# Eight wide matmuls first, then eight narrow ones, in each output tile of the first product

## The reference, cut to what matters

```python
w = weight[adapter_ids]                       # (8, 1024, 1024), one matrix for each of 8 sequences
c = jnp.einsum('bsi,boi->bso', x, w)          # the first product: x (8, 256, 1024)
logits = c @ W_router.T                       # 8 experts, softmax, top 2, renormalised: combine
h = jnp.einsum('nd,erd->ner', c, A_stack) * combine[..., None]
lora = jnp.einsum('ner,eor->no', h, B_stack) * SCALING
out = x + c @ W_base.T + b_base + lora        # all float32
```

## Time and profile before

| | us |
|---|---|
| median of 3 runs | 419.95 (419.89 to 420.39) |
| profiled execution, its own time | 421.21 |
| its span, first to last instruction | 419.4 |
| TensorE busy | 407.3 (97%) |
| wide matmuls L798, 512 of them | mean 405 ns |
| narrow matmuls L800, 512 of them | mean 283 ns |
| DVE busy | 303.9 (72%) |
| ACT busy | 187.5 (45%) |

### The profile page before, as it was taken

The page is one execution under the profiler, slowest core; times in us unless marked ns, Lnnn a source line. Parts: engine busy times, 40 slices in busy tenths (PEclk is TensorE's granted clock), DMA queues, the critical chain, the costliest instruction groups (busy, mean ns, idle before and its releaser), DMA issues.

```text
span 419.4 us, 5350 instructions
## 1 busy us (share of the span) xinstructions
PE 407.3 (97%) x2010; PEld 341.9 (82%) x2010; DVE 303.9 (72%) x435; ACT 187.5 (45%) x289; POOL 39.8 (9%) x67
## 2 busy tenths in 40 slices
PE   7589999999999999999999999999999999999996
PEld 6478888888888888888888888888888888888885
DVE  2388794787979999877447688468877999987321
ACT  3387663474873234313126577246667224431100
POOL 8000000000000013012127000000000002201110
PEclk9689999999999999999999999999999999999999
DMA  7999685065813015467549959416444202631221
GB/s 238 363 362 324 207 288 187 31 221 166 299 38 100 2 75 168 159 210 273 185 168 322 391 174 327 157 60 198 146 161 155 86 2 80 197 127 50 100 77 75
DMA packets 21930, 72.84 MB, mean 174 GB/s; under 512 B 2912, under 2 KB 3952, under 8 KB 21904
## 3 DMA queue, kind: packets, MB, share of 16 engines
q1 hardware_dynamic: 16704, 56.11, 39.6%
q0 software_dynamic: 4912, 15.87, 10.7%
q10 hardware_dynamic: 288, 0.52, 0.4%
HBM read 64.10 MB, written 8.39 MB: 173 GB/s over the span
## 4 chain that ended last, share of the span: by engine, by line
PE 94%; DMA 3%; SPq 1%; DVE 0%; issue 0%; ACT 0%
PE bank_x L798 28%; PE bank_x L800 14%; PE bank_y L774 9%; PE bank_y L776 8%; PE bank_y L775 8%; PE bank_x L774 7%; PE bank_x L776 7%; PE bank_x L775 7%; DMA raw<-w_cond 3%; PE bank_y L813 2%; PE bank_y L814 2%; SPq L332 1%; PE bank_y L837 0%; SPq L344 0%; PE bank_y L829 0%
## 5 line engine op out<-in xcount | busy, mean ns | idle before, releaser
L798 PE MATMUL bank_x<-x_hl,wc_hl 128*128 128x512 f32 x512 | 185.3, 405 | 7.6 <-DVE wc_hl L648 5.9
L800 PE MATMUL bank_x<-x_hl,wc_hl 128*128 128x256 f32 x512 | 145.0, 283 | 0.0
L526 DVE TENSOR_TENSOR wc_hl<-raw,wc_hl 128x1024 fp32r<-128x1024 f32 x90 | 108.8, 1220 | 23.3 <-ACT wc_hl L452 23.3
L798 PEld LDWEIGHTS bank_x<-x_hl,wc_hl 128*128 128x128 f32 x512 | 97.8, 191 | 33.7 <-DVE wc_hl L648 6.5
L452 ACT CAST wc_hl<-raw 128x1024 fp32r<-128x1024 f32 x90 | 94.0, 1051 | 66.7 <-PE bank_y L776 34.8
L800 PEld LDWEIGHTS bank_x<-x_hl,wc_hl 128*128 128x128 f32 x512 | 98.5, 192 | 0.1
L406 POOL DMA_DIRECT2D out<-out_sb x28 | 15.3, 546 | 362.9 <-DVE out_sb L577 341.4
L569 DVE SCALAR_TENSOR_TENSOR out_sb<-bank_x,bias_sb,out_sb 128x512 f32<-128x512 f32 x32 | 23.8, 747 | 24.5 <-PE bank_x L776 19.1
L490 ACT COPY xc_low<-bank_x 128x256 f32<-128x256 f32 x64 | 23.7, 370 | 33.5 <-PE bank_x L800 33.5
L774 PE MATMUL bank_x<-x_hl,wc_hl 128*128 128x512 f32 x96 | 37.4, 389 | 0.0
L776 PE MATMUL bank_x<-x_hl,wc_hl 128*128 128x512 f32 x96 | 37.4, 389 | 0.0
(11 more groups left out here) (94 smaller groups left out, 511.2 us busy)
## 6 DMA issues: line engine op xcount, KB each, us to landing
raw<-w_cond SPq DMA_DIRECT2D x62, 512.0 KB, 4.5
raw<-w_base SPq DMA_DIRECT2D x24, 512.0 KB, 5.0
out_sb<-x POOLq DMA_DIRECT2D x32, 256.0 KB, 5.5
raw<-x SPq DMA_DIRECT2D x14, 512.0 KB, 4.5
out<-out_sb POOLq DMA_DIRECT2D x28, 256.0 KB, 2.3
raw<-w_cond SPq DMA_DIRECT2D x8, 128.0 KB, 7.2
out<-out_sb SPq DMA_DIRECT2D x4, 256.0 KB, 2.0
raw<-x ACTq DMA_DIRECT2D x2, 256.0 KB, 2.8
```

The costliest lines, as they stand in the source:

```text
L526: nc.vector.tensor_tensor(split_dst(key, LO), split_src(key), split_dst(key, HI).bitcast(F32), ALU.subtract).then_inc(lo_done, 1)
L798: nc.tensor.matmul(ps[:], wc_hl[:, w, HI, k], x_hl[:, s % 2, k].rearrange("p h n -> p (h n)"), start=(k == 0), stop=False)
L800: mm = nc.tensor.matmul(ps[:, TOK:], wc_hl[:, w, LO, k], x_hl[:, s % 2, k, HI], start=False, stop=(k == KT - 1))
```

## The change

In every tile but the first two, TensorE now waits only for the high part of the weights, does the eight wide matmuls, then waits for the low part, and does the eight narrow ones. The bank, the operands, the number of matmuls and weight loads and the increment at the end stay as they are. Tiles (0,0) and (0,1) keep their turns.

```diff
             def cond(s, t):
                 starts = s == 0 and t < 2
                 if not starts:
-                    pe.wait_ge(lo_done, SPLIT["w", s, t])
+                    pe.wait_ge(hi_done, SPLIT["w", s, t])
...
                     nc.tensor.matmul(ps[:], wc_hl[:, w, HI, k], x_hl[:, s % 2, k].rearrange("p h n -> p (h n)"),
                                      start=(k == 0), stop=False)
-                    mm = nc.tensor.matmul(ps[:, TOK:], wc_hl[:, w, LO, k], x_hl[:, s % 2, k, HI],
-                                          start=False, stop=(k == KT - 1))
+                    if starts:
+                        mm = nc.tensor.matmul(ps[:, TOK:], wc_hl[:, w, LO, k], x_hl[:, s % 2, k, HI],
+                                              start=False, stop=(k == KT - 1))
+                if not starts:
+                    pe.wait_ge(lo_done, SPLIT["w", s, t])
+                    for k in range(KT):
+                        mm = nc.tensor.matmul(ps[:, TOK:], wc_hl[:, w, LO, k], x_hl[:, s % 2, k, HI],
+                                              start=False, stop=(k == KT - 1))
                 mm.then_inc(cond_done, 1)
```

## The result

| | before | after |
|---|---|---|
| median of 6 runs, us | 420.46 (419.89 to 420.99) | 416.40 (416.06 to 416.75) |
| ratio | | 0.9904, 95% interval 0.9892 to 0.9917 |
| profiled execution, its own time | 421.21 | 416.06 |
| its span | 419.4 | 414.3 |

The change is worth 4.1 us. Predicted were 414.6 (411.0 to 418.8) and a gain of 5.4; the profiled pair is 5.15 apart, the medians 4.06. The prediction started from the median of the first three runs of before, 419.95. With three more it is 420.46, so of the 1.8 us between 414.6 and 416.40, 0.5 lies in the starting point and 1.3 in the gain.

A forecast was written before the change was run, and what follows sets the result against it. TensorE was taken as the bound: a start paced by loads and splits, then a stream of matmuls each costing its spacing. 1.27 + 0.81 + 0.28 + 3.0 = 5.4 us off the median 419.95 gave 414.6, range 411.0 to 418.8.

The forecast's parts named there:

- The wait of tile (0,2): In tile (0,2), wide matmuls start when the high part is made, not the low part: 1.27 us earlier.
- The clock: In tile (0,2), a busier TensorE avoids the half clock; half of 1.62 us taken, 0.81.
- The wait of tile (3,3): Ahead of tile (3,3), the wait for DVE's low part and the restart behind it go: 0.28 us.
- The order: In tiles behind (0,2), narrow behind narrow takes 0.120, so 56 tiles go from 2.827 to 2.773: 3.0 us.
- The added waits: Two waits per tile ahead of its loads, hidden by the running matmul, cost nothing; uncovered, 6.7 us for 61 tiles.
- From the profile to the median: Whole kernel: the same terms, 5.4 us, taken from the profiled 421.21 (415.8) and from the median 419.95 (414.6).
- weight loads that can't keep the pace: Narrow runs: loads of 0.19 stretch the spacing beyond 0.120; at 0.135 the kernel takes 421.9; chance 0.10.
- the quicker narrow spacing: Narrow runs: narrow behind narrow takes 0.113, a gain of 8.7 us in all, to 411.3; chance 0.17.
- The order does nothing: All reordered tiles: narrow ones keep 0.127, tiles stay at 2.83, gain 2.1 us, to 417.9; chance 0.25.

The follow-up runs named there:

- Experiment 4: Changed kernel with tile (0,2) waiting for the low part before its first matmul: bare, ratio 0.9951; with eight matmuls on zeros ahead of that wait, 0.9935.
- experiment 1: Changed kernel's matmul order in all 62 tiles, but each waits for the low part before its first matmul, as in the kernel before; ratio 0.9970.
- e8_late02: Changed kernel, except that tile (0,2) waits for the low part before its first matmul; ratio 0.9951.
- experiments 3 and 6: Kernel before plus eight matmuls on zeros ahead of tile (0,2), ratio 0.9996; kernel before plus one ahead of each of five tiles, one execution, no time given.
- experiments 2 and 3: Kernel before with only tile (0,2) in the new order and wait, 0.9966; kernel before plus eight matmuls on zeros ahead of (0,2), 0.9996.
- experiment 7: Kernel before with tiles (0,2), (3,3) wide first on the high part and a zero matmul ahead of five tiles, 418.30; changed kernel again beside it, 416.91.

## Why the prediction was right, and where its terms were off

The direction and the range held, and so did the mechanism: all four terms are there. Their sizes were right in two of them, and that the sum came close is partly luck. By its own steps, against the profiled pair (5.1 us of span):

- **The wait of tile (0,2), 1.27.** Held: it started at 22.00, released by L452, 1.45 before 23.45, of which 0.20 is that ACT's copy began earlier in this profile (20.90 for 21.10). Experiment 4 has 1.3 for it, sure to 1 us.
- **The clock, 0.81 as half of 1.62.** The pair has the whole of it: (0,3) starts 3.02 earlier, of which the two terms in full are 2.89. In the medians about half fits: 7 of 12 executions in experiment 1 and 4 of 10 in `e8_late02` lie in the upper heap. For the kernel before itself the share is not known, since its executions vary in the gait too. "Half" was a guess. The argument behind it, that TensorE would be busier ahead of the tile, fits the pair (3.19 of 3.80 us), but the clock also stayed in a profile with 1.14 (experiment 4), so it does not say when the clock falls.
- **The wait of tile (3,3), 0.28.** Held: (3,2) and (3,3) take 2.79 each and 0.31 less together than before, 0.01 of it by the order. DVE makes the low part of (3,3) by 102.41 (101.19 + 1.22), but the tile starts at 102.04, so 0.37 us of waiting are covered there by the wide matmuls:

```profile
101.19 1.22 DVE L526 TENSOR_TENSOR wc_hl<-raw,wc_hl 128x1024 fp32r<-128x1024 f32 x1 [0.52 <-ACT wc_hl L452]
102.04 0.86 PE L798 MATMUL bank_x<-x_hl,wc_hl 128*128 128x512 f32 x3
```

- **The order, 3.0.** This term was mis-sized: it measured 56 x (2.827 - 2.793) - 5 x 0.020 = 1.8, of it 1.1 in the 32 tiles of the second group, where 1.7 was forecast. The narrow spacing that it took, 0.120, was right (0.119 to 0.120 in the trace). What the step left out is the turn: "A tile is then 8 x (0.2267 + 0.120)" counts the wide ones behind narrow ones as if they came behind wide ones. They cost 0.028 more a tile, of which the narrow ones give 0.008 back. The sign was there: in the slow gait of before a narrow one started 0.237 behind its wide one in the mean and the wide one 0.117 behind the narrow, in the quick gait 0.232 and 0.115. Neither has a wide spacing of 0.2267, so taking 0.2267 off a pair did not measure a narrow one; that 0.120 came out is luck. By the Trainium skill ("TensorE: Matmul & The Clock Gate", section "Back-to-back issue gap") the gap of a matmul taken by itself is N/2.4 + 2.5 ns, 0.109 for a narrow one; that section does not claim it for a stream with a weight load ahead of each matmul, as the prediction used it. The trace has 0.120 in such a stream, and the measurement decides.
- **The added waits, nothing.** Held: eight narrow ones take 0.95 with the wait ahead of them, and no wait for L526 is in the list.
- 1.27 + 1.62 + 0.28 + 1.8 = 5.0, against 5.1. The prediction's 5.4 was close because the clock was too small by 0.81 and the order too large by 1.2.
- **From the profile to the median.** The same 5.4 was taken off the median. The medians moved by 4.1, because the profiled execution of before (421.21) lay 0.75 above its median and that of the changed kernel (416.06) 0.34 below its own. The former had the half clock in (0,2) and the slow gait in 56 of 61 tiles; that these two put it above the median is likely, but the traces of the others are not there to show it. Two other profiles with turns go partly in the quick gait (experiments 3 and 6), in which the new order would lose 0.020 a tile.

Of the rivals, weight loads that can't keep the pace are out, since the narrow ones go at 0.12, and so is the quicker narrow spacing. "The order does nothing" is out in the profiles, though it gives less than half of the gain.

## What to carry to other kernels

When a product needs its operand in two parts, do first all the work that needs only the part that is ready first: the second part's latency then lies under it. Cost the reordering of a matmul stream by spacings in the very neighbourhood that it will have, a wide one behind a narrow one too, and not by one taken from a uniform stream. Before a term goes from a profiled execution to the median, ask whether it is in all executions: a stretch of half clock or a gait of the stream may be in some of them only.

## What the runs showed of the hardware that I had not expected

- The same alternating stream of matmuls of 512 and 256 columns runs at 2.827 or 2.773 us for 16, keeps its pace for up to 15 tiles, and changes it only where something breaks the stream (a wait in (3,3), one extra matmul of 0.06 us ahead of (2,4), the router behind (1,7)). Not every break does it: the same wait in (3,3) left the pace at 2.83 in experiments 2 and 3, and so did three of the five added matmuls in experiment 7.
- Runs of one, two, four and eight give 2.773 or 2.827, 2.787, 2.800 or 2.807, and 2.793: not monotonic.
- Of the same kernel, tile (0,2) started at 22.00 in one profile and at 24.06 in another, by the arrival of the loads (22.93 instead of 20.87 for its own weights). That is more than the order of the matmuls is worth (1.8).
- The clock fell to 0.50 behind a wait of 1.65 us in the kernel before, and stayed at 1.00 behind one of 2.13 in `e8_late02`. What tells the two apart is open.
